# Attention with tiles of two rings taking turns on TensorE, and the products with V in up to four blocks

## What is computed

```python
# first attention: 16 heads of 16, window of 128 tokens to either side
energy = jnp.einsum('bhqd,bhkd->bhqk', q, k)
energy = jnp.where(out_of_window, fmin, energy)
att = jax.nn.softmax(energy / scaling, axis=-1)
out = jnp.einsum('bhqk,bhkd->bhqd', att, v)
...
# second attention: blocks of 64 tokens; each block of queries sees its own block,
# its two neighbours, the first and the last; the first and last blocks see all keys
aw = jax.nn.softmax(band, axis=-1)
mid_ctx = jnp.einsum('bhlqk,bhlkd->bhlqd', aw[..., wn:4 * wn], exp_v)
```

## Time and profile before

| | |
|---|---|
| median of 3 runs | 2556.39 us (2556.25 to 2556.92) |
| the profiled execution | 2556.15 us, its span 2554.4 us |
| first attention, first to last exponential | 205.9 to 730.6 us |
| second attention, first to last exponential | 1807.3 to 2412.5 us |
| PE, DVE, ACT busy over the span | 2271.2, 1853.9, 1670.1 us |

### The profile page before, as it was taken

One profiled execution on the slowest core, in us unless ns is written; L12 is line 12 of the kernel. 1 busy time (PEld: TensorE's weight loads), 2 busy tenths in 40 slices (PEclk: granted clock), 3 DMA queues, 4 the chain that ended last, 5 costly groups with the idle time before them and its releaser, 6 DMA issues. The chain is left out here.

```text
span 2554.4 us, 73394 instructions
## 1 busy us (share of the span) xinstructions
PE 2271.2 (89%) x25549; PEld 1358.6 (53%) x25549; DVE 1853.9 (73%) x5631; ACT 1670.1 (65%) x3892; POOL 1075.1 (42%) x1338
## 2 busy tenths in 40 slices
PE   6979999999979588859999994987999999999875
PEld 4633333333326477748888884553344444444354
DVE  5549999999927577644444444774999999999297
ACT  6946888888842455514454443773688888888743
POOL 3533555555559477736666663442000000000075
PEclk9978999999979799979999997997799999999978
DMA  7452333333232466635654334684232232222152
GB/s 232 178 185 70 86 79 87 85 84 84 68 86 75 108 179 185 165 114 126 137 130 106 92 90 132 215 269 148 55 73 75 74 79 68 76 76 66 44 161 93
DMA packets 363697, 289.65 MB, mean 113 GB/s; under 512 B 228400, under 2 KB 296752, under 8 KB 363344
## 3 DMA queue, kind: packets, MB, share of 16 engines
q1 hardware_dynamic: 349616, 248.24, 36.3%
q0 software_dynamic: 12960, 35.60, 4.0%
q10 hardware_dynamic: 768, 1.12, 0.2%
HBM read 133.53 MB, written 123.69 MB: 101 GB/s over the span
## 5 line engine op out<-in xcount | busy, mean ns | idle before, releaser
L707 ACT ACTIVATE a_pr<-a_pst 128x384 f32<-128x384 f32 (+3 forms) x2176 | 917.0, 484 | 163.2 <-PE a_pst L742 137.3
L655 DVE TENSOR_REDUCE a_mx<-a_psc 128x1 f32<-128x384 f32 (+2 forms) x1152 | 574.3, 565 | 32.9 <-PE a_psc L742 20.4
L742 PE MATMUL a_psc<-a_ke,a_qe 52*128 52x128 f16 (+5 forms) x3072 | 539.3, 287 | 46.5 <-DMA a_ke<-mrow 30.7
L806 PE MATMUL a_po<-a_pr,a_ve 128*17 128x128 f32 (+3 forms) x10496 | 562.6, 302 | 2.0 <-ACT a_pr L707 1.2
L650 DVE CUSTOM_DVE_ANT_0 a_cut<-a_psc,row_mask 128x384 bf16<-128x384 f32 (+1 forms) x1024 | 478.3, 521 | 44.4 <-PE a_psc L742 27.0
L742 PE MATMUL a_pst<-a_qe,a_ke 53*128 53x128 f16 (+5 forms) x3072 | 439.7, 283 | 2.8 <-ACT a_pr L707 0.6
L629 POOL TENSOR_SCALAR_AFFINE_SELECT a_pr<-a_pr 128x512 f32<-128x512 f32 x448 | 276.0, 637 | 294.5 <-ACT a_pr L707 294.5
L742 PEld LDWEIGHTS a_psc<-a_ke,a_qe 52*128 52x128 f16 (+1 forms) x3072 | 223.7, 95 | 210.4 <-DVE a_mx L650 92.1
L742 PEld LDWEIGHTS a_pst<-a_qe,a_ke 53*128 53x128 f16 (+1 forms) x3072 | 153.5, 94 | 320.8 <-ACT a_pr L707 206.4
L1877 POOL TENSOR_TENSOR x_res<-x_res,t_att 128x512 f32<-128x512 f32 x32 | 40.0, 1272 | 674.0 <-DVE t_att L1906 674.0
L806 PEld LDWEIGHTS a_po<-a_pr,a_ve 128*17 128x17 f32 x10496 | 193.7, 96 | 194.0 <-issue 137.6
(11 more groups left out here) (234 smaller groups left out, 4264.4 us busy)
## 6 DMA issues: line engine op xcount, KB each, us to landing
a_qe<-qx SPq DMA_DIRECT2D x378, 64.0 KB, 2.6
a_ke<-kx SPq DMA_DIRECT2D x378, 64.0 KB, 2.7
vx<-p_vst SPq DMA_DIRECT2D x32, 544.0 KB, 3.2
a_ve<-vx SPq DMA_DIRECT2D x64, 272.0 KB, 3.1
qx<-p_stg SPq DMA_DIRECT2D x64, 256.0 KB, 3.3
kx<-p_stg SPq DMA_DIRECT2D x64, 256.0 KB, 3.1
ox<-a_ost SPq DMA_DIRECT2D x256, 64.0 KB
x_res<-x SPq DMA_DIRECT2D x16, 512.0 KB, 8.9
```

What stands on the lines that cost most here:

```text
L655: dve.tensor_reduce(out.unsqueeze(1), psc[(u * n_s + n) % RING][:, 0:width], AXX, ALU.max)\
L707: act.activation(pr[s % SLOTS][:, h // 2, h % 2, 0:width], pst[prob_slot(u, n) % RING][:, 0:width], ACT.Exp, scale=scale).then_inc(p_ready, 1)
L742: last = pe.matmul(out[:, col:col + count], stat, mov(tok, count), start=(k == 0), stop=(k == len(pieces) - 1), skip_group_check=True, til ...
L806: last = pe.matmul(po[h][32 * a:32 * a + VW, tok % CH:tok % CH + w], ve[g][:, t, a * VW:(a + 1) * VW], pr[s % SLOTS][:, a // 2, a % 2, col ...
```

## The change

`score_pair` and `prob_pair` are replaced by `score_tile` and `prob_tile`, which make one tile. `step` goes through the four heads of a job one by one: probability tile n, score tile n, then a quarter of the products with V. The score tiles take the halves of the array in the other order (`par = 1 - n % 2`), so that the probability tile and the score tile of the same n lie on different halves; VectorE's outputs are indexed to match. Piece n of a job with k pieces stands in part `n * 4 // k`: with two pieces these are parts 0 and 2 (after the first and the third tile), with three pieces parts 0, 1 and 2. No job has four.

```diff
             def maxima(g, b):
                 u = unit(g, b)
                 for n in range(n_s):
-                    j, h = divmod(n, 4)
-                    par, i = h % 2, h // 2
+                    j, par, i = n // 4, 1 - n % 2, n // 2 % 2
...
-            def score_pair(g, b, n):
...
-                for par in range(2):
-                    after(pe, s_read, u * n_s + n + par - RING + 1)
-                    product(par, psc[(u * n_s + n + par) % RING], qe[g][rows(par, KS), i, t * P:(t + 1) * P],
-                            lambda tok, count: ke[g][rows(par, KS), i, tok:tok + count], pieces, s_ready)
+            def score_tile(g, b, n):
+
+                u, par = unit(g, b), 1 - n % 2
+                j, i = n // 4, n // 2 % 2
...
+                after(pe, s_read, u * n_s + n - RING + 1)
+                product(par, psc[(u * n_s + n) % RING], qe[g][rows(par, KS), i, t * P:(t + 1) * P],
+                        lambda tok, count: ke[g][rows(par, KS), i, tok:tok + count], pieces, s_ready)
...
+            def prob_tile(g, b, n):
+
+                u, par = unit(g, b), n % 2
+                s, i = n // 4, n // 2 % 2
...
+                free_to(pe, k - RING)
+                product(par, pst[k % RING], ke[g][rows(par, KR), i, t * P:(t + 1) * P],
+                        lambda tok, count: qe[g][rows(par, KR), i, tok:tok + count], pieces, t_ready)
...
-                middle = (len(pieces) + 1) // 2
...
-                    if (n < middle) == (part == 0):
+                    if n * 4 // len(pieces) == part:
...
+                        if n == len(pieces) - 1:
+                            last.then_inc(p_used, 1)
...
-                if part == 1:
-                    last.then_inc(p_used, 1)
...
-                    for i in range(2):
-                        n = 4 * s + 2 * i
+                    for h in range(4):
+                        n = 4 * s + h
                         if n == K_TURN and after_cur:
                             turn(*after_cur)
-                        prob_pair(*cur, n)
+                        prob_tile(*cur, n)
                         if nxt:
-                            score_pair(*nxt, n)
+                            score_tile(*nxt, n)
                         if s >= LAG:
-                            with_v(*cur, s - LAG, i)
+                            with_v(*cur, s - LAG, h)
```

More of the change, by code:

```diff
@@ L744, in product @@
                 last.then_inc(ready, 1)
-            def score_pair(g, b, n):
-                u = unit(g, b)
-                j, h = divmod(n, 4)
-                i = h // 2
+            def score_tile(g, b, n):
+                u, par = unit(g, b), 1 - n % 2
+                j, i = n // 4, n // 2 % 2
                 t, pieces, _m = jobs[j]
@@ L809, in with_v @@
                                              tile_position=(0, 32 * a))
+                        if n == len(pieces) - 1:
+                            last.then_inc(p_used, 1)
                     opened.add(h)
-                if part == 1:
-                    last.then_inc(p_used, 1)
             def scores(g, b):
-                for n in range(0, n_s, 2):
-                    score_pair(g, b, n)
+                for n in range(n_s):
+                    score_tile(g, b, n)
             def start():
@@ L826, in step @@
                 for s in range(nj):
-                    for i in range(2):
-                        n = 4 * s + 2 * i
+                    for h in range(4):
+                        n = 4 * s + h
                         if n == K_TURN and after_cur:
                             turn(*after_cur)
-                        prob_pair(*cur, n)
+                        prob_tile(*cur, n)
                         if nxt:
-                            score_pair(*nxt, n)
+                            score_tile(*nxt, n)
                         if s >= LAG:
-                            with_v(*cur, s - LAG, i)
+                            with_v(*cur, s - LAG, h)
                         elif prev:
-                            with_v(*prev, nj - LAG + s, i)
+                            with_v(*prev, nj - LAG + s, h)
             def end(last):
                 for s in range(nj - LAG, nj):
-                    for part in range(2):
+                    for part in range(4):
                         with_v(*last, s, part)
```

## The result

The changed kernel takes 2655.86 us (median of 4 runs, 2652.51 to 2670.6) against 2556.32 us before: a ratio of 1.0391, 95% interval 1.0371 to 1.0411. The prediction had 2655 us in a range of 2610 to 2702. The profiled execution took 2659.12 us, its span is 2657.4 us, 103.0 us longer than the one before.

A forecast was written before the change was run, and what follows sets the result against it. The prediction took a loop through V blocks, tile 3 and its exponential to bound the second stage, VectorE's pace mostly the first. 2556.15 + 126 (second stage) - 27 (first) = 2655 us, range 2610 to 2702.

The forecast's parts named there:

- the V loop: Second stage: first V block, tiles, tile 3, its exponential, next first V block; 22.9 us a unit, +126 us.
- from the exponential of tile 3 to the block: Second stage: start of tile 3's exponential to the V block that waits for it, 0.65 us.
- Two of its signs: Second stage, changed profile: VectorE idle 4 to 5 us a unit; ScalarE idle about 1 us a job.
- The period of the first stage: First stage mostly at VectorE's pace of 14.8 plus small waits: 15.65 us a unit against 16.50, -27 us.
- the 0.35 of the sum: First stage: V blocks' wait for GpSimd behind the short jobs, 0.35 us a unit.
- the bound of the second stage: High bound: each of 18 tile steps loads its weights in the open, 1.4 us a unit more, +171 us.
- the V loop already sets the pace: Kernel before, 384-wide second-stage jobs: no V block starts until tile 3's exponential is done; 1.98 us a job.
- the smoother order wins: Rival, both stages: the first block's wait ends before TensorE comes to it; 2484 us, chance 0.05.
- The V loop did not reach the first stage: Rival: it rules there too, every job waits; +10 us in place of -27, 2692 us, chance 0.10.
- The drop of the clock: Rival, second stage: TensorE at 1.2 not 2.4 GHz for a tenth of it; 32 us, total 2687, chance 0.05.
- the clock falls only after the engine has idled for a time: TensorE, second stage: the skill's clock rule, cited against the rival of a falling clock.
- a fourth block: Rival that the change doesn't do what it says: no job has four pieces; already in the sum, no chance given.

The follow-up runs named there:

- second experiment: Kernel before the change, with the second attention's products with V two jobs back instead of one (four exponential buffers): 2558.95 us, 1.0016 of before.
- the half of the change that is smoother: The change with only the tiles taking turns, V blocks left where they stood before (behind tiles 1 and 3): 2507.24 us, 0.9814 of before.
- the first experiment: The change with the second attention's products with V two jobs back instead of one (four exponential buffers instead of three): 2539.63 us, 0.9933 of before.

## Why the prediction was right

- **What bounds the second stage of the changed kernel** was right: the V loop, with its place (first block waits for tile 3's exponential, tile 3 stands behind all blocks) and its parts. Taking the wait out, moving the blocks by one tile, and joining two of them moved the period as the loop says. The measured 2.50 us against 2.59 summed has one mis-sized term: from the exponential of tile 3 to the block, 0.65 was taken from the earlier trace rows, and it took 0.55. In the earlier trace rows the block stood behind a score tile, not behind that exponential (second experiment). Over one unit of the changed kernel, jobs 0 to 8 take 2.82, 2.43, 2.16, 2.49, 2.50, 2.49, 2.50, 2.36 and 2.41 us from first block to first block, where the prediction had 2.82, 2.46, 2.25, four times 2.59, 2.52 and 2.52. The term is right for job 0 and 0.1 too long in most others; job 7 is 0.16 under its sum, since the tile steps of a 320-wide job are shorter too (blocks 0.59 apart, not 0.62). Together that is the 0.8 us between 22.9 and 22.15.
- **Two of its signs came out smaller.** VectorE was to be idle 4 to 5 us a unit in the second stage, and is idle 2.8 (busy 174.3 of 200 us in the stretch shown below); ScalarE was to be idle about 1 us a job, and is idle 0.5 (busy 159.0 of 200). VectorE's busy time went up with the longer period (549.1 to 580.9 us over the stage).
- **The period of the first stage** was right: 15.7 us a unit against 15.65 forecast. Its terms weren't tested one by one. In the changed kernel the profile puts 14.1 us in 63 waits of V blocks down to GpSimd, 0.44 us a unit, near the 0.35 of the sum; but the one run on them (three jobs back) speaks against that wait in the version with the blocks behind tiles 1 and 3.
- **That the median fell within 1 us of the forecast is partly luck.** In the second stage 0.75 us a unit too much was forecast, 24 us in all. About as much came from two places that weren't in the sum. First, the second stage got 118 us longer between its first and last exponential, of which the steady difference of 3.2 us a unit explains 102; most of the other 16 is the clock of TensorE at the end of the stage (below; 14 us by the estimate there). Second, the first stage got 17 us shorter and not 27. In part this is the clock too, which came to 1.00 later at its start, as the same ten microseconds show, before and in the changed kernel:

```profile
218.00:228.00 10.00, 9.79 (x139) 4.02 (x137) 9.16 (x42) 8.37 (x22) 4.86 (x9) 1.00 0.14 39
```
```profile
218.00:228.00 10.00, 10.00 (x100) 2.31 (x92) 6.77 (x28) 5.97 (x14) 3.66 (x6) 0.50 0.01 2
```

  The unit made there took 21.9 us by VectorE's once-a-unit operation, 17.7 before. Whether the change has to do with that wasn't tested. The four runs of the changed kernel lie between 2652.5 and 2670.6 us, so a single run could have missed by 15 us. The upper end of the range was added up with 160 us where the bound of the second stage is 171; with 171 it is 2713, and nothing hangs on it.
- **What was wrong** is the reading of the kernel before: "the V loop already sets the pace". With the loop taken out, the wide jobs kept their 1.98 us. What moved them was TensorE's order behind a V block: with the first score tile 0.17 or 0.18 us behind the probability tile they took 1.98, in two different orders of the tiles, and with both side by side 1.86. The prediction had used this for the first stage only. It made no difference to the sum, since the second stage before was taken as measured.
- **The rivals.** That the smoother order wins is right for the half of the change that is smoother: alone it gives 2507 us. The V loop did not reach the first stage: that wanted 16.8 us a unit, and it is 15.7. The drop of the clock was in the right stage, at its end only, and cost about 14 us by estimate, not 32. The prediction's reading, that the clock falls only after the engine has idled for a time, doesn't fit it: TensorE's longest listed wait in the 19 us before the fall was 0.8 us. No job got a fourth block.

## What to carry to other kernels

When a block of work waits for the last item of the batch before it, count what stands on the same in-order queue between that block and the item that the next block will wait for: all of it is in the loop, and splitting the block finer and spreading it puts more into it. Spread such work only behind the item that is awaited, or let it wait for older data. A releaser named for a short wait isn't proof: take the dependence away and see whether the period moves.

## What the runs showed of the hardware

Two products on different halves of the array's rows start together (2107.60 and 2107.60 in the rows of the changed kernel); on the same half the second starts 0.18 us later (2076.03 and 2076.21, tiles of 384 columns). That placement alone is 43 us of this kernel (2549.9 against 2507.2).

TensorE's granted clock stayed at 1.00 through most of the second stage, with TensorE busy 84% of the time. It fell to 0.50, so from 2.4 to 1.2 GHz, in the last two units, in which no score tiles are left. Three stretches of the changed kernel, two of the kernel before, and the end of the stage in the first experiment (the change with the products with V two jobs back):

```profile
2100.00:2300.00 200.00, 168.52 (x2827) 67.40 (x2821) 174.31 (x346) 159.04 (x352) 0.00 (x0) 1.00 0.26 63
...
2440.00:2463.00 23.00, 19.20 (x315) 7.41 (x313) 12.80 (x26) 18.24 (x41) 0.00 (x0) 1.00 0.09 16
2464.00:2490.00 26.00, 21.89 (x212) 5.36 (x204) 0.00 (x0) 14.55 (x32) 0.00 (x0) 0.50 0.10 18
```
```profile
2377.00:2396.00 19.00, 18.23 (x267) 7.46 (x270) 2.44 (x6) 17.93 (x44) 0.00 (x0) 1.00 0.10 17
2396.00:2413.00 17.00, 15.97 (x246) 6.46 (x244) 0.00 (x0) 15.76 (x38) 0.00 (x0) 1.00 0.11 19
```
```profile
2376.00:2394.00 18.00, 18.00 (x270) 6.75 (x265) 0.00 (x0) 17.17 (x41) 0.00 (x0) 1.00 0.10 18
```

All of them do the same work there. The kernel before kept the clock to its last exponential, and so did the first experiment, which has the blocks of the change without its wait, and the runs with the blocks behind tiles 1 and 3 and behind tiles 1, 2 and 3. The changed kernel lost it, and so did the run with two blocks behind tiles 0 and 2, the other one that keeps the wait (0.50 in its last 31 us of the stage). So the drop goes with the waits for ScalarE on top of the thinner work. In the changed kernel ScalarE then got 32 operations done in 26 us, after 41 in 23 us at the full clock, and against 38 in the last 17 us of before. The 60 operations from 2464 to 2512 took 48 us; at 41 in 23 us they would have taken 34, so the drop cost about 14 us, an estimate.

The four runs of the changed kernel spread over 18 us. The first four of the kernel before spread over 0.7, but 13 runs of it beside the experiments over 8.5 (2551.4 to 2559.9). In the changed kernel and in the run with two blocks the mean granted clock falls as the time rises: 0.935 at 2652.5 and 0.928 at 2670.6 us in the one, 0.944 at 2601.5 and 0.931 at 2616.3 us in the other. That the spread comes from when the clock falls is likely, but wasn't tested.
